# Small products in row and column groups, and the gate/up low-rank product added to the weights

## The chip, the cores and the metric

The kernel runs on one core of one Trainium2 chip. The metric is the device time of one execution in microseconds, of which the median of several runs is taken. One profiled execution gives the rows that are read here; its time is told beside its span.

## What is computed

The reference is two decoder layers on 8 x 128 = 1024 tokens of width 512, each step followed by a residual sum and a layer norm. Cut to what the change touches:

```python
# layer 1, "attention" (quantised weights with low-rank additions)
def _lin_lora(x, W, A, B):                 # A: (16, in), B: (out, 16)
    base = jnp.einsum('bsh,oh->bso', x, W)
    lora = jnp.einsum('bsr,or->bso', jnp.einsum('bsh,rh->bsr', x, A), B)
    return base + lora
q, k, v = (_lin_lora(x, _dequant(codes[n], scales[n]), A[n], B[n]) for n in range(3))
o  = _lin_lora((q + k + v) / 3.0, _dequant(codes[3], scales[3]), A[3], B[3])
x1 = x + o
g  = _lin_lora(x1, _dequant(codes_gu[0], scales_gu[0]), A[4], Bgu[0])   # 512 -> 1792
u  = _lin_lora(x1, _dequant(codes_gu[1], scales_gu[1]), A[5], Bgu[1])   # 512 -> 1792
h  = jax.nn.silu(g) * u
return x1 + _lin_lora(h, _dequant(codes_down, scales_down), A_down, B_down)
# layer 1, cross attention: scores = (x Wq^T + bq)(ctx Wk^T + bk)^T / sqrt(512), softmax, times ctx
```

Before it come layer 0 (an attention of eight heads of width 8, a softmax over the channels of the context, a linear layer with one of four low ranks chosen per token), and behind it the cross attention and a feed-forward layer with ternary weights.

## The kernel before

The 1024 tokens are eight tiles of 128 (NT = 8). Each engine has its own program, written out by hand in one order, and waits for counters (semaphores) that the others raise; what stands behind a waiting instruction in its engine's program waits as well. In the line numbers below L502 is the helper that transposes a token tile, L1023 ScalarE's copy of a transposed tile, L1430 VectorE's low half of it.

**Early parts.** The keys of the cross attention are prepared while the eight heads are worked on: `key_step` (L590 to L608) makes Wk^T Wq in four groups of four products and then two rows, bk Wq and bq Wk, each as four products with one output row, accumulated. In the next loop `key_bias` (L655) makes the bias row of the keys for half of the tokens, again four accumulated products of one output row and 512 columns; ScalarE copies it (L1141), and one DMA writes it out. In the third loop `attention_lora` (L732) makes the low-rank part of the four attention weights, two products a step (48 rows of contraction for q, k, v together, 16 for o), and VectorE adds each (`add_lora`, L1570). Products of float32 operands are two instructions each in the trace.

**The token loop (L817).** Step t holds: `attention_out(t)` (L763, four products of 512 columns), the transposes of tile t - 1 from `rbuf` (L502), and two `down_lora` products (L804, contraction 16, 512 columns) that VectorE adds to the down weights in `fold` (L1672). VectorE's loop (L1639) adds x1 (L1646), takes the low half of the transposed tile (L1430), at step 0, 1, 2 and 5 joins and scales weights (L1359, L1365, L1377, L1600), at step 4 makes the first tile's low half (L1605), sums x1 (L1668) and makes its folds. From the second step on TensorE's `attention_out(t)` waits for the x1 sum two steps back, the transposes for the one before.

**The gate/up stage (L847 to L851).** It has 14 tiles (j) of 128 gate and 128 up columns, two buffers (s = j mod 2). ScalarE bends codes into values (L973 to L989), VectorE joins and scales them; ScalarE rounds the weights to float32r (`gu_hi`, L1166) and VectorE takes what is left (`gu_low`, L1605). TensorE then runs, for each half of the tokens (tg, 512 columns) and for gate and up, twelve products high x high, high x low, low x high, and one for the low rank:

```python
pe.matmul(dst, b_st[:, s, g * P:(g + 1) * P], th[:, cols], start=False, stop=True).then_inc(done, 1)
```

Its operand `th` is x1 A^T, made between the token loop and the first tile by `gu_lora` (L807, 24 products for both halves), rounded by ScalarE (L1186) and completed by VectorE (L1637). `b_st` is B, rounded tile by tile (L1170, L1610) from `b_gu`, which SyncE loads. ScalarE applies silu to the gate's bank (L1198), VectorE multiplies by the up bank (`hidden`, L1595). TensorE may overwrite a pair of banks (gate and up of one half) when the hidden product of four pairs before is done:

```python
pe.wait_ge(h_ready, 2 * j + tg + 1)     # four pairs of banks in turn, the count starts at 4
```

VectorE's order in a tile is `gu_rest` (join_below, scale), `hidden` of the tile two back, `gu_join_above` of the next tile, the low half of B, `gu_low`. The down product follows (L859), which uses banks 0 to 7 for the eight token tiles.

## Time and profile before

| what | us |
|---|---|
| median of 3 runs (739.55 to 745.03) | 739.68 |
| profiled execution, its own time | 739.51 |
| its span, first to last instruction | 737.7 |
| busy: TensorE, VectorE, ScalarE | 691.8, 398.7, 384.4 |

The busy shares tell which engine is short; the chain tells which work ended last, step by step backward. The duration of one product in the trace holds its way through the array, which overlaps with the next product, so the distance between starts is its price, not its duration. The granted clock is given as a share of full speed: 1.00 is 2.4 GHz and 0.50 is 1.2 GHz.

### The profile page before, as it was taken

The numbers are of one execution on the slowest core, as the hardware profiler recorded it, in microseconds if no ns is written. First come the engines' busy times: TensorE is split into PE (matmuls) and PEld (weight loads), VectorE is DVE, ScalarE is ACT, GpSimd is POOL, SyncE is SP. The second block draws the span as 40 slices with busy tenths as digits, with TensorE's granted clock in tenths as the row PEclk, the third lists the DMA queues.
The fourth block names the chain that finished last, engine by engine and source line by source line (L and its number), as shares of the span: only waits on it lengthen the run. The fifth ranks groups of instructions, "written<-read, shape, count | busy, mean of one in ns | idle before, by whom it ended". The sixth has DMA issues, their size and how long they took to land.

```text
span 737.7 us, 8504 instructions
## 1 busy us (share of the span) xinstructions
PE 691.8 (94%) x3196; PEld 480.7 (65%) x3196; DVE 398.7 (54%) x691; ACT 384.4 (52%) x553; POOL 66.9 (9%) x126
## 2 busy tenths in 40 slices
PE   5879999999999998999999999999997999999993
PEld 3545454544554446888888887888764888887872
DVE  3367776657556773665555623456677222223386
ACT  4456677945557506757575713444434333334653
POOL 1022213201112000000000000002122000000022
PEclk9889999999999799999999999999999999999997
DMA  5582095421123320332423000003450122210002
GB/s 154 200 295 80 3 283 168 135 71 58 61 60 112 92 63 18 107 104 85 122 77 115 5 1 0 1 1 114 157 230 28 58 58 85 66 50 0 0 29 85
DMA packets 24905, 63.32 MB, mean 86 GB/s; under 512 B 5471, under 2 KB 10143, under 8 KB 23970
## 3 DMA queue, kind: packets, MB, share of 16 engines
q1 hardware_dynamic: 24866, 62.79, 26.7%
q8 instruction: 25, 0.41, 0.2%
q14 instruction: 14, 0.11, 0.0%
HBM read 58.06 MB, written 4.72 MB: 85 GB/s over the span
## 4 chain that ended last, share of the span: by engine, by line
PE 84%; DVE 7%; ACT 4%; issue 2%; DMA 2%; POOL 1%; SPq 1%; POOLq 0%; DVEq 0%; ACTq 0%
PE bank L859 16%; PE bank L842 7%; PE bank L843 7%; PE bank L844 7%; PE bank L928 7%; PE bank L929 7%; PE bank L722 4%; PE bank L763 4%; PE bank L652 3%; PE bank L502 2%; PE bank L750 2%; PE bank L845 2%; PE bank L804 2%; PE bank L602 1%; PE bank L578 1%
## 5 line engine op out<-in xcount | busy, mean ns | idle before, releaser
L981 ACT ACTIVATE line<-line 128x1024 f32<-128x1024 f32 x87 | 91.1, 1048 | 0.1
L928 PE MATMUL bank<-xh,wh 128*128 128x512 f32 x224 | 88.4, 395 | 1.5 <-issue 1.5
L859 PE MATMUL bank<-wh,xh 128*128 128x512 f32 x224 | 87.8, 392 | 2.0 <-DVE xl L1689 1.8
L842 PE MATMUL bank<-xh,wh 128*128 128x512 f32 x224 | 87.8, 392 | 1.4 <-DVE th L1637 1.4
L929 PE MATMUL bank<-xl,wh 128*128 128x512 f32 x224 | 88.1, 393 | 0.0
L843 PE MATMUL bank<-xl,wh 128*128 128x512 f32 x224 | 87.5, 391 | 0.0
L859 PE MATMUL bank<-wh,xl 128*128 128x512 f32 x224 | 87.4, 390 | 0.0
L844 PE MATMUL bank<-xh,wl 128*128 128x512 f32 x224 | 87.4, 390 | 0.0
L1332 POOL TENSOR_SCALAR rstd<-mv 128x1 f32<-128x1 f32 x45 | 20.0, 445 | 650.7 <-DVE mv L1703 474.9
L1222 ACT ACTIVATE xh<-arena 128x512 fp32r<-128x512 f32 x56 | 35.4, 632 | 68.5 <-PE bank L859 59.8
L1689 DVE TENSOR_TENSOR xl<-arena,xh 128x512 fp32r<-128x512 f32 x56 | 38.5, 688 | 52.5 <-ACT xh L1222 52.3
L1789 DVE SCALAR_TENSOR_TENSOR arena<-bank,ff_s,arena 128x512 f32<-128x512 f32 x28 | 21.0, 751 | 79.1 <-PE bank L929 77.7
L1595 DVE TENSOR_TENSOR arena<-arena,bank 128x512 f32<-128x512 f32 x28 | 19.2, 685 | 60.3 <-PE bank L845 60.3
L859 PEld LDWEIGHTS bank<-wh,xh 128*128 128x128 f32 x224 | 42.0, 188 | 13.0 <-DVE xl L1689 3.3
L928 PEld LDWEIGHTS bank<-xh,wh 128*128 128x128 f32 x224 | 42.6, 190 | 10.5 <-issue 1.7
L842 PEld LDWEIGHTS bank<-xh,wh 128*128 128x128 f32 x224 | 42.2, 188 | 10.9 <-DVE th L1637 1.9
L929 PEld LDWEIGHTS bank<-xl,wh 128*128 128x128 f32 x224 | 42.6, 190 | 8.9
L843 PEld LDWEIGHTS bank<-xl,wh 128*128 128x128 f32 x224 | 42.2, 189 | 9.1
L844 PEld LDWEIGHTS bank<-xh,wl 128*128 128x128 f32 x224 | 42.0, 188 | 9.2
L859 PEld LDWEIGHTS bank<-wh,xl 128*128 128x128 f32 x224 | 42.1, 188 | 8.6
L1198 ACT ACTIVATE arena<-bank 128x512 f32<-128x512 f32 x28 | 16.6, 591 | 57.8 <-PE bank L845 57.8
L1359 DVE SCALAR_TENSOR_TENSOR line<-line 128x1024 f32<-128x1024 f32 x29 | 35.3, 1216 | 18.5 <-ACT line L989 18.4
(183 smaller groups left out, 1202.6 us busy)
## 6 DMA issues: line engine op xcount, KB each, us to landing
codes<-in_c_gu SPq DMA_DIRECT2D x14, 512.0 KB, 3.9
scales<-in_s_gu SPq DMA_DIRECT2D x28, 256.0 KB, 3.8
codes<-in_t_gu SPq DMA_DIRECT2D x14, 512.0 KB, 3.6
codes<-in_c_dn SPq DMA_DIRECT2D x7, 512.0 KB, 4.8
scales<-in_s_dn SPq DMA_DIRECT2D x14, 256.0 KB, 3.9
fold<-in_t_dn SPq DMA_DIRECT2D x1, 3584.0 KB, 13.3
codes<-in_c_qkv SPq DMA_DIRECT2D x6, 512.0 KB, 4.9
arena<-in_xT SPq DMA_DIRECT2D x4, 512.0 KB, 4.9
```

The costliest lines, as they stand in the source:

```text
L722: pe.matmul(bank[FF_BANK[b % 3]][:, :], xT[:, k, b * P:(b + 1) * P], w0T[:, k, :], start=(k == 0), stop=False)
L763: last = pe.matmul(turn_bank(t)[:, :], xT[:, k, t * P:(t + 1) * P], mT[k], start=(k == 0), stop=(k == KD - 1))
L842: pe.matmul(dst, wh[:, s, c:c + P], xh[:, k, cols], start=(k == 0), stop=False)
L843: pe.matmul(dst, wh[:, s, c:c + P], xl[:, k, cols], start=False, stop=False)
L844: pe.matmul(dst, wl[:, s, c:c + P], xh[:, k, cols], start=False, stop=False)
L859: last = pe.matmul(bank[b][:, :], h[:, s, b * P:(b + 1) * P], wp[:, s, 0:D], start=first and p == 0, stop=last_one and p == len(parts) - 1)
L928: pe.matmul(dst, wh[:, s, c:c + P], xh[:, k, cols], start=(k == 0), stop=False)
L929: last = pe.matmul(dst, wh[:, s, c:c + P], xl[:, k, cols], start=False, stop=(k == KD - 1))
L981: nc.scalar.activation(below(slot), below(slot), ACT.Prelu, bias=bias, scale=scale, alpha=alpha).then_inc(bent, 1)
L1222: nc.scalar.activation(xh[:, s, cols], hT[:, slice(j, j + 1), cols].rearrange("p o t -> p (o t)"), ACT.Copy).then_inc(done, 1)
L1359: nc.vector.scalar_tensor_tensor(weight(slot), weight(slot), FAR_NEAR, near(slot), ALU.add, ALU.max).then_inc(joined, 1)
L1689: return nc.vector.tensor_tensor(xl[:, s, cols], hT[:, slice(j, j + 1), cols].rearrange("p o t -> p (o t)"), f32(xh[:, s, cols]), ALU.subt ...
```

## The change

**Gate and up.** `th`, `b_st`, `ah`, `al` and all their steps are gone. In their place TensorE makes the low-rank weights themselves, A^T B of a tile (`gu_lora(j)`): four float32 products with 32 rows of contraction and 256 columns, in row groups 0 and 1, into banks 2 and 3. VectorE adds both banks to the scaled weights in one step (`gu_lora_add`, in `gu_rest`) before they are rounded, and ScalarE's rounding waits for the addition. Tiles 0 and 1 have theirs in steps 1 and 4 of the token loop, the others at the head of the tile before. Since banks 2 and 3 are taken, three pairs of banks go in turn (`pair_bank`), and a pair waits for the hidden product of three pairs before. `late_bank` turns the bank numbers of all that follows by two.

**Down fold.** Three `down_lora` products a step lie in three row groups (steps 0 to 4; before, two a step in steps 0 to 6) and wait together for all folds of the step before. **Attention.** The two `attention_lora` products of a step are one for q, k, v in rows 0 to 63 and one for o in rows 64 to 127. **Key rows.** The products of one output row in `key_step` and `key_bias` go to four column groups and are no longer accumulated; the copy takes 128 rows, and the four parts are summed later by a product with `picked` or with `ones` of four rows. The bias row is written by four DMAs in place of one.

```diff
+GU_LORA = (1, GU1_STEP - 1)
-X3_BANK = (7, 4)
+X3_BANK = (1, 6)
+PAIR_BANK = (0, 4, 6)
...
+        lora_ps = heads_ps[:, 0:2, :]
+        def pair_bank(p, g):
+            return bank[PAIR_BANK[p % len(PAIR_BANK)] + g][:, :]
+        def late_bank(n):
+            return bank[(n + 2) % len(bank)]
...
@@ SyncE
+            for c in range(KD):
+                sp.dma_start(beta_dram[c:c + 1, :], beta_s[c * ROWG:c * ROWG + 1, :]).then_inc(kb_out, 16)
...
                     sp.dma_start(codes[:, slot, :],
                                  i["c_gu"][slice(j, j + 1), :, :].rearrange("o p c -> (o p) c")).then_inc(in_gu[s], 16)
+                    if j >= 2:
+                        sp.wait_ge(lora_made, j - 1)
+                    sp.dma_start(b_gu[:, s, :], i["b_gu"][j]).then_inc(in_bgu[s], 16)
                     sp.wait_ge(scaled, C_GU + j - RING + 1)
...
-                    sp.wait_ge(b_ready, j + 1)
-                    sp.dma_start(b_gu[:, s, :], i["b_gu"][slice(j, j + 1), :, :].rearrange("o r c -> (o r) c")).then_inc(in_gus[s], 16)
@@ TensorE: key_step, key_bias
-                    last = pe.matmul(bank[0][0:1, :], k_b[:, d:d + 1], wq1[:, d, :], start=(d == 0), stop=(d == KD - 1))
+                    last = pe.matmul(bank[0][d * ROWG:d * ROWG + 1, :], k_b[:, d:d + 1], wq1[:, d, :], start=True, stop=True)
...
-                    last = pe.matmul(bank[7][0:1, :], wb[:, KD + c:KD + c + 1], ctxT[:, g, c, :], start=(c == 0), stop=(c == KD - 1))
+                    last = pe.matmul(bank[7][c * ROWG:c * ROWG + 1, :], wb[:, KD + c:KD + c + 1], ctxT[:, g, c, :], start=True, stop=True)
@@ attention_lora
-                if n >= 2:
-                    pe.wait_ge(af_added, n - 1)
-                j = n % KD
-                rows = slice(0, 3 * R1) if n < KD else slice(O_ROW, O_ROW + R1)
+                j, o = divmod(n, 2)
+                if n >= 2 and not o:
+                    pe.wait_ge(af_added, n)
+                rows = slice(o * O_ROW, (o + 1) * O_ROW)
@@ down_lora, gu_lora, token loop
-                if j >= 3:
-                    pe.wait_ge(fold_kept, j - 2)
-                rows = slice(QR * (j // DT), QR * (j // DT) + R1)
+                if j >= 3 and j % 3 == 0:
+                    pe.wait_ge(fold_kept, j)
+                rows = slice(QR * (j % 3), QR * (j % 3) + R1)
...
-            def gu_lora(tg):
-                pe.wait_ge(a_ready, 1)
-                pe.wait_ge(xl_ready, NT // 2 * (tg + 1))
-                for k in range(KD):
-                    for a, xs in ((ah, xh), (ah, xl), (al, xh)):
-                        last = pe.matmul(bank[2 + tg][0:3 * RG, :], a[:, k, :], xs[:, k, tg * 512:(tg + 1) * 512],
-                                         start=(k == 0 and a is ah and xs is xh), stop=(k == KD - 1 and a is al))
-                last.then_inc(t_ps, 1)
+            def gu_lora(j):
+                pe.wait_ge(in_bgu[j % 2], 16 * (j // 2 + 1))
+                if j == 0:
+                    pe.wait_ge(in_agu, 16)
+                    pe.wait_ge(ln_sum, 3 * NT)
+                else:
+                    pe.wait_ge(lora_added, j)
+                for h in range(2):
+                    for n in range(2):
+                        rows = slice(n * RG, (n + 1) * RG)
+                        last = pe.matmul(lora_ps[:, n, h * 2 * P:(h + 1) * 2 * P], a_gu[rows, h, :], b_gu[rows, j % 2, :], start=True, stop=True)
+                last.then_inc(lora_made, 1)
...
-                for j in range(2 * t, min(2 * t + 2, NF)):
+                for j in range(3 * t, min(3 * t + 3, NF)):
                     down_lora(j)
-                if t == NT - 1:
-                    gu_lora(0)
-            gu_lora(1)
+                if t in GU_LORA:
+                    gu_lora(GU_LORA.index(t))
@@ gu_tile
                 pe.wait_ge(w_ready, j + 1)
-                pe.wait_ge(b_ready, j + 3)
+                if 1 <= j < NF - 1:
+                    gu_lora(j + 1)
...
-                    pe.wait_ge(h_ready, 2 * j + tg + 1)
+                    p = TG * j + tg
+                    if p == 0:
+                        pe.wait_ge(xl_ready, NT // 2)
+                    elif p == 1:
+                        pe.wait_ge(xl_ready, NT)
+                        pe.wait_ge(fold_kept, NF)
+                    else:
+                        pe.wait_ge(h_ready, p + 2)
...
-                        pe.matmul(dst, b_st[:, s, g * P:(g + 1) * P], th[:, cols], start=False, stop=True).then_inc(done, 1)
@@ ScalarE
-                if t == 2:
-                    act.wait_ge(in_agu, 16)
-                    nc.scalar.activation(ah[:, :, :], aT_gu, ACT.Copy).then_inc(a_hi, 1)
...
-                act.wait_ge(scaled, C_GU + j + 1)
+                act.wait_ge(lora_added, j + 1)
                 nc.scalar.activation(wh[:, s, :], weight(gu_slot(s)), ACT.Copy).then_inc(hi_ready, 1)
@@ VectorE
+            def gu_lora_add(s, j):
+                dve.wait_ge(lora_made, j + 1)
+                dve.wait_ge(scaled, C_GU + j + 1)
+                w = weight(gu_slot(s)).rearrange("p (h i c) -> p i h c", h=2, i=2)
+                nc.vector.tensor_tensor(w, w, lora_ps.rearrange("p i (h c) -> p i h c", h=2), ALU.add).then_inc(lora_added, 1)
...
                 gu_scale(s, n)
+                gu_lora_add(s, j)
...
-                gu_lora_low(s, j)
...
-                for j in range(2 * b, min(2 * b + 2, NF)):
+                for j in range(3 * b, min(3 * b + 3, NF)):
                     dve.wait_ge(fold_ready, j + 1)
```

## Rows read from the trace of the kernel before

**Rows 1.** The page: busy time, share and instructions; the chain by engine.

```profile
PE 691.8 (94%) x3196; PEld 480.7 (65%) x3196; DVE 398.7 (54%) x691; ACT 384.4 (52%) x553; POOL 66.9 (9%) x126
...
PE 84%; DVE 7%; ACT 4%; issue 2%; DMA 2%; POOL 1%; SPq 1%; POOLq 0%; DVEq 0%; ACTq 0%
```

**Rows 2.** Windows view, gate/up stage: busy us of each engine and count, clock, DMA.

```profile
286.00:453.00 167.00, 166.36 (x727) 136.89 (x728) 84.75 (x92) 102.47 (x130) 0.00 (x0) 1.00 0.24 70
```

**Rows 3.** Timeline, TensorE in the first tile: start us, us, engine, line, operands.

```profile
289.27 0.39 PE L844 MATMUL bank<-xh,wl 128*128 128x512 f32 x1
...
289.50 0.40 PE L845 MATMUL bank<-th,b_st 96*128 96x512 f32 x1
...
289.73 0.40 PE L842 MATMUL bank<-xh,wh 128*128 128x512 f32 x1
```

**Rows 4.** Timeline, TensorE between the token loop and the first tile.

```profile
276.93 0.60 PE L502 MATMUL bank<-ident,rbuf 128*128 128x128 f32 x4
...
277.29 0.48 PE L813 MATMUL bank<-xh,ah 128*96 128x512 f32 x1
...
286.64 0.50 PE L842 MATMUL bank<-xh,wh 128*128 128x512 f32 x1 [1.40 <-DVE th L1637]
```

**Rows 5.** Timeline around the first key_bias: TensorE, then ScalarE's idle time behind it.

```profile
116.90 3.59 PE L660 MATMUL bank<-project,wb 128*1 128x512 f32 x8
...
120.43 1.12 PE L637 MATMUL bank<-heads,prob 128*128 128x512 f32 x2
...
125.02 0.69 ACT L1113 ACTIVATE heads<-bank,wb 128x512 f32<-128x512 f32 x1 [3.19 <-PE bank L652]
```

**Rows 6.** Timeline, small float32 products in column groups (L567), then row groups (L539).

```profile
58.31 0.62 PE L567 MATMUL bank<-fold 128*32 128x128 f32 x16
58.87 0.73 PE L539 MATMUL bank<-heads 9*128 9x128 f32 x16
59.52 1.98 PE L602 MATMUL bank<-arena 128*128 128x512 f32 x4
```

**Rows 7.** Timeline, one step of the token loop: transposes, down products, attention_out.

```profile
264.98 0.60 PE L502 MATMUL bank<-ident,rbuf 128*128 128x128 f32 x4
...
265.51 1.98 PE L804 MATMUL bank<-arena 16*128 16x512 f32 x4
...
267.42 3.70 PE L763 MATMUL bank<-arena 128*128 128x512 f32 x8
```

**Rows 8.** Timeline, VectorE in the token loop: two folds, scale, addition.

```profile
236.17 1.27 DVE L1672 TENSOR_TENSOR fold<-fold,bank 128x512 f32<-128x512 f32 x2
...
250.24 1.22 DVE L1600 SCALAR_TENSOR_TENSOR line<-line,scales 128x1024 f32<-128x1024 f32 x1
...
251.38 0.68 DVE L1668 TENSOR_TENSOR x<-x,rbuf 128x512 f32<-128x512 f32 x1
```

**Rows 9.** Timeline, VectorE in a gate/up tile: hidden product and low half.

```profile
310.81 0.69 DVE L1595 TENSOR_TENSOR arena<-arena,bank 128x512 f32<-128x512 f32 x1 [3.80 <-PE bank L845]
...
313.89 1.23 DVE L1605 TENSOR_TENSOR wl<-line,wh 128x1024 fp32r<-128x1024 f32 x1
```

**Rows 10.** The page: granted clock in 40 slices; windows view of one stretch.

```profile
PEclk9889999999999799999999999999999999999997
...
240.00:244.00 4.00, 4.00 (x6) 1.71 (x6) 3.12 (x5) 1.47 (x2) 0.00 (x0) 0.50 0.32 94
```

**Rows 11.** Timeline, one attention_lora step (two products, four instructions).

```profile
161.38 1.98 PE L741 MATMUL bank<-heads,arena 48*128 48x512 f32 x4
```

**Rows 12.** Timeline, the rounding of A for gate and up, TensorE behind.

```profile
51.71 0.56 DVE L1517 TENSOR_TENSOR al<-fold,ah 128x384 fp32r<-128x384 f32 x1 [0.55 <-ACT ah L1097]
...
53.46 0.44 PE L546 MATMUL bank<-ident,fold 128*128 128x128 f32 x2 [1.08 <-DVE fold L1465]
```

**Rows 13.** Timeline, key_step with the seventh token tile, and VectorE's maximum.

```profile
85.29 1.88 PE L604 MATMUL bank<-arena,k_b 128*1 128x512 f32 x4
...
86.04 1.21 DVE L1465 TENSOR_REDUCE fold<-bank 128x8 f32<-128x1024 f32 x1
```

More of the change, by code:

```diff
@@ L139, in decoder_kernel @@
         wl = sb("wl", [P, 2, CH], F32R)
[L140 to L146 removed]
+        b_gu = sb("b_gu", [2 * RG, 2, 2 * P])
+        a_gu = sb("a_gu", [2 * RG, 2, P])
+        folded_m = sb("folded", [P, T])
         ff_s = sb("ff_s", [P, 2, 2])
@@ L286, in decoder_kernel @@
         in_gus = [sem(f"in_gu_scales{n}") for n in range(2)]
+        in_bgu = [sem(f"in_b_gu{n}") for n in range(2)]
         in_ctx1, in_kq, in_wk, in_wq, in_ds = sem("in_context1"), sem("in_kq"), sem("in_wk"), sem("in_wq"), sem("in_ds")
@@ L1437, in _ @@
             nc.vector.memset(lmT[RMAX:RMAX + 1, :, :], 1.0)
-            link(nc.vector.memset(ones[:, :], 1.0))
+            nc.vector.memset(wb[:, 2 * KD:2 * KD + 1], 0.0)
+            nc.vector.memset(ones[:, :], 1.0)
+            link(nc.vector.memset(picked[:, :], 0.0))
+            for c in range(KD):
+                nc.vector.memset(picked[c * ROWG:c * ROWG + 1, :], 1.0)
             for g in range(HG):
@@ L1871, in layout @@
         "s_o": pairs(sa[3].T.reshape(KD, 2, D)), "lora_l": lora_l, "lora_r": lora_r,
-        "aT_gu": rows(np.tile(A[4:6].reshape(RG, D).T, 3)), "b_gu": b_gu, "a_d": a_d, "bT_d": bT_d,
+        "a_gu": c(A[4:6].reshape(RG, 2, 2, P).transpose(2, 0, 1, 3).reshape(2 * RG, 2, P)), "b_gu": b_gu, "a_d": a_d, "bT_d": bT_d,
         "c_gu": wide(f["L1_attn_codes_gu"][0], f["L1_attn_codes_gu"][1]),
```

135 lines of the change are left out of this document (49 added, 86 removed).

## The prediction

> **What bounds the kernel now.** I read the page's busy shares first, then its chain: TensorE is busy 94% of the span and holds 84% of the chain that ended last, the other engines about half busy [rows 1]. So a step is worth what it takes off TensorE's queue, or off a wait in which TensorE stands. Then I read the stages. In the gate/up stage 727 products are recorded in 167.0 us with 166.36 busy [rows 2]: nothing but TensorE limits it. The duration printed for one product (0.39 to 0.40 us) is no price, since products overlap: starts lie 0.23 apart [rows 3]. 166.36 / 727 = 0.2288 us each is the price I use; with 0.395 the removed product would look worth 22.1 us in place of 12.8.
>
> **Prices of small float32 products.** A float32 product is two instructions. Eight of them, 512 columns each, take 116.90 to 120.43 [rows 5], so 0.44 apiece, and so 0.22 for 256 columns (half the columns). Where small products already lie in groups, sixteen instructions of 128 columns in four row groups go from 58.87 to the next product at 59.52, 0.65 us, and sixteen in column groups from 58.31 to 58.87, 0.56 us [rows 6]; one behind the other they would take 16 x 0.11 = 1.76. So groups do run beside each other here. The change uses two, three or four groups, and 256 or 512 columns, which no row shows; between full overlap (the longest one counts) and none (they add up) I take full overlap, as rows 6 are nearest.
>
> A switch between whole-array and grouped products costs something. Four transposes before a whole-array product start 0.36 ahead of it [rows 4]; before the 16-row products of the down fold they start 0.53 ahead, so 0.17 goes into the switch; behind it four instructions take 265.51 to 267.42, 1.91 for 4 x 0.44 = 1.76, so 0.15 comes out [rows 7]. A visit to grouped mode costs 0.32. The Trainium skill, page "TensorEngine Tiling (Array Packing)", section Key Properties, says that changing the tiling mode drains TensorE, without a figure, which speaks against visits in the middle of a dense stream; the rows agree with 0.32 a visit, and a sum with no drain would come out 12 x 0.32 = 3.8 us lower.
>
> **Gate/up stage.** Removed: L845, 56 products x 0.2288 = 12.8 us. Added at the head of tiles 1 to 12: one visit with two halves of two row groups, 4 x 0.22 + 0.32 = 1.20 us, x 12 = 14.4 us (no overlap at all: 8 x 0.22 + 0.32 = 2.08, 25.0 us; no drain and full overlap: 0.88, 10.6 us). The stage becomes 1.6 us longer, between 2.2 shorter and 12.2 longer. It gains nothing by itself.
>
> A tile is then 48 x 0.2288 + 1.20 = 12.2 us. New waits: VectorE adds the low-rank tile from PSUM (1024 columns; 512 cost about 0.64 in a pair [rows 8], so 1.25) only after the visit for it, at the start of the tile before; behind that wait on VectorE's queue lie the two hidden products of the tile two back, join_above and gu_low; on ScalarE gu_hi waits for the addition. From the start of a tile: visit done 1.3, addition 2.6, hidden products 3.3 and 4.0, ScalarE's rounding 3.7, join_above 5.2, gu_low (1.23 [rows 9]) 6.5. Who waits: TensorE's second pair, which with three pairs of banks in turn needs the hidden product of three pairs before, at 1.2 + 5.5 = 6.7 (there at 3.3), and the next tile at 12.2 (there at 6.5). Slack 3.4 and 5.7 us, and VectorE idles 3.8 before a hidden product today [rows 9]; ScalarE loses 0.4 a tile with b_st. I cost these waits at nothing. SyncE's b_gu load now waits for the visit two tiles back, a tile ahead of its use; nothing.
>
> **Between the token loop and the first tile.** Now the last transposes are at 276.93, half of the x-by-A products from 277.29, and the tile stream starts at 286.64, behind the second half and the rounding of it on ScalarE and VectorE [rows 4]. All of that goes. But the token loop before is rearranged too, so I laid it out again, in the clock of this trace, with attention_out 8 x 0.44 = 3.5, transposes 0.4, VectorE's additions 0.64 to 0.69 and its 1024-wide steps 1.22 [rows 7, 8]. Down products now come in threes (0.88 + 0.32 a step in place of 1.91 + 0.17), and a step's three wait for all folds of the step before. Step 0 runs three from 234.5; VectorE's folds of step 0 end 238.1 (three, from 236.17 [rows 8]), and TensorE waits 1.9 us for them; then three products and gu_lora(0), attention_out(2) at 240.2 as today. VectorE's step 1 (three additions, one scale, three folds) ends 244.0; its step 2 holds both joins, the scale, the new addition and three folds, and ends 253.0. TensorE's fourth group waits for that from 249.3: 3.7 us idle. Then attention_out(4) to 257.5, two products and gu_lora(1), attention_out(5) to 263.5. VectorE's step 5 with the second tile's weights ends 271.0, steps 6 and 7 carry two additions and x_low each, the last transposes are at 274.4, and the stream starts at 274.9. It needs only half of xl there; the other half is wanted 5.5 us later and is there in 1.5. Tile 1's weights: ScalarE's four bends and rounding end 280.7, VectorE 282.2, wanted 285.9; covered.
>
> So 286.64 - 274.9 = 11.7 us, if the clock stays at 2.4 GHz. Today it is at 1.2 GHz (0.50) for all of 240 to 244 and falls twice in 237 to 258 by the page's digits [rows 10]; the first fall follows 16-row products and small waits. With idle stretches of 1.9 and 3.7 us I keep one fall of 3.4 us, which costs 1.7: 10.0 us gained. Bounds 6 (waits as laid out, two long falls) and 12.
>
> **Earlier parts.** key_bias, twice: eight instructions in 3.53 [rows 5] become four column groups in 2 x 0.44 + 0.32 = 1.20, 2.33 saved each. TensorE goes straight on into context and keys; ScalarE, next latest, idles 3.19 behind it today [rows 5]: 4.7 us, bounds 2.3 and 5.3. attention_lora, four times: four instructions in 1.9 [rows 11] become two in time, 0.88 saved each, switches unchanged: 3.5 us, bounds 0 and 3.5; VectorE's work in a step (about 7.1) is near TensorE's new period but not above it. The rounding of A at 51: VectorE's part, waiting for ScalarE's, ends at 52.2 and TensorE idles 1.08 for the row maximum behind it [rows 12]: 1.0 saved, bounds 0 and 1.1. key_step's last two groups: four instructions take 1.88 [rows 13], but behind them TensorE waits for VectorE's maximum, done 87.25, so the first pair saves nothing; the second saves some 0.6, and the single ones pay about as much for switches: 0, bounds -1 and +1. The copies of 128 rows in place of 1 have the same columns; three more SyncE issues for beta, the memsets and the turned bank numbers have slack: nothing.
>
> **Sum.** -1.0 - 4.7 - 3.5 - 10.0 + 1.6 = -17.6 us. The profiled execution took 739.51 (span 737.7 and 1.8 around it), the median of the runs shown is 739.68: 739.5 - 17.6 = 721.9 us.
>
> **Rivals.** (a) The visits in the tile stream overlap badly (256 columns with a weight load in the same row group each time), the rest as forecast: +10.6, 732.5. For it: no row shows it with two groups; against it: rows 6. (b) Slower: groups do not overlap at these column counts anywhere. Then gate/up is 12.2 longer, key_bias is longer by a switch (0.6 in all), attention_lora saves nothing, and the token loop loses four of its ten: -1.0 + 0.6 - 6.0 + 12.2 = +5.8, 745.3. It decides from the point where less than about a quarter of the overlap is there (the overlap is worth 23.4 us in all, and 5.8 of that is missing for a draw). Against it stand both rows of grouped products [rows 6]. (c) VectorE's blocked queue: if the hidden product behind the addition came 3.4 us later than laid out, the second pair would wait; each further microsecond costs 12. At 1 us over: 734. (d) The token loop gives less: VectorE and TensorE in lockstep with two clock falls, 726. (e) More: fewer falls also around 155 and 180 and no drain in the stream, 714.
>
> **Chances.** Forecast 0.58, (a) 0.12, (b) 0.03, (c) 0.04, (d) 0.15, (e) 0.08. The range takes in forecast, (d) and (e) with their bounds and leaves out (b), (c) and the end of (a): 713 to 731. A change within 1% (732.1 to 747.1) is about what a measurement of this kernel cannot tell from none. Faster by over 1%: forecast, (d), (e) and half of (a) and more, 0.90; within 1%: 0.08; slower: 0.02.
>
> **What would show it.** Groups of the visit: four pairs of starts some 0.22 apart, and 1.2 between the products around them, else (a). Starts of tiles 12.2 apart, with no wait for a hidden product (else c). The tile stream starting 11.7 or 10 us earlier against attention_out(0), with TensorE waits for the folds near its second and fourth group. L660's successor about 1.2 behind it. The prediction is wrong if the gate/up stage is not within 164 to 179 us, or if VectorE makes the token loop longer than laid out.

## The result, and the profile after

The median after the change is 721.09 us (720.24 to 722.53, four runs), before it 740.06 on the same chip; the ratio is 0.9735, with a 95% interval of 0.9696 to 0.9774. Faster by 2.65%, 0.8 us from the forecast of 721.9 and inside the range. The profiled execution took 721.29 (span 719.5); before it was 739.51 (737.7), so 18.2 us are to be found. Of all executions reported in this document one stood far from the others of its kernel (key_bias_row, 1723.13 us), and no ratio counts it.

The page first. TensorE still holds 81% of the chain [rows 1 had 84%], so marks on its queue split the difference. The clock row ends in a 7 in both kernels: in the last 8.6 us (before) and 9.3 us (after) of the span TensorE has no product left and its granted clock is 1.2 GHz.

```profile
PE 668.8 (93%) x3228; PEld 468.4 (65%) x3228; DVE 404.9 (56%) x694; ACT 379.6 (53%) x536; POOL 66.9 (9%) x126
PEclk9979999999999899999999999999999999999997
PE 81%; DVE 8%; ACT 4%; issue 2%; DMA 2%; POOL 1%; SPq 1%; POOLq 0%; DVEq 0%; ACTq 0%
```

Then the stretches between the marks, kernel after. A row gives the stretch and its length, then the busy time of TensorE, of its weight loads, of VectorE, ScalarE and GpSimd, then the granted clock and the DMA traffic. The marks are the first of the single-row key products (L612), the two key_bias, attention_lora, attention_out(0), the first product of the gate/up stream and the first down product:

```profile
79.40:117.40 38.00, 35.16 (x240) 18.93 (x240) 28.89 (x50) 28.92 (x42) 8.78 (x12) 0.96 0.65 194
117.40:141.10 23.70, 23.70 (x99) 13.05 (x97) 16.39 (x36) 21.44 (x35) 7.62 (x14) 1.00 0.44 145
141.10:155.20 14.10, 12.47 (x49) 5.86 (x48) 8.68 (x26) 8.48 (x13) 1.61 (x4) 1.00 0.36 113
155.20:215.20 60.00, 59.27 (x210) 30.17 (x209) 38.32 (x125) 36.89 (x51) 7.14 (x19) 1.00 0.24 72
215.20:268.40 53.20, 45.05 (x150) 20.65 (x148) 42.25 (x57) 23.36 (x28) 3.95 (x4) 0.90 0.25 73
268.40:436.30 167.90, 167.90 (x770) 133.44 (x769) 90.95 (x92) 100.20 (x118) 0.00 (x0) 1.00 0.23 67
```

The stretch from attention_out(0) to the stream, which this text calls the loop, was this in the kernel before:

```profile
226.50:286.60 60.10, 57.08 (x157) 25.74 (x155) 42.38 (x59) 25.93 (x33) 3.93 (x4) 0.91 0.24 66
```

The clock column has to be read before the lengths. Up to that last idle end, TensorE's granted clock is 1.2 GHz in both kernels for stretches of 3.4, 6.8 or 10.2 us and 2.4 GHz otherwise; a product takes twice as long there (starts of the down products of down_one_group lie 0.85 apart at 1.2 GHz and 0.43 at 2.4), so 3.4 us at the lower level cost about 1.7. Kernel before, then kernel after, for their low stretches behind 79 us (before had 20.4 us there, after 13.6; ahead of 79 us both have 13.6):

```profile
155.60:159.00 3.40, 3.40 (x7) 1.58 (x6) 2.89 (x14) 0.00 (x0) 0.00 (x0) 0.50 0.53 158
179.50:182.90 3.40, 3.40 (x7) 1.33 (x6) 3.19 (x16) 1.93 (x3) 1.11 (x3) 0.50 0.00 0
237.50:244.30 6.80, 6.80 (x9) 2.50 (x8) 4.16 (x6) 3.97 (x5) 0.00 (x0) 0.50 0.24 66
254.60:258.00 3.40, 3.40 (x5) 1.35 (x4) 1.65 (x3) 0.83 (x1) 0.00 (x0) 0.50 0.09 19
572.00:575.40 3.40, 3.40 (x10) 2.62 (x9) 0.75 (x1) 1.15 (x4) 0.00 (x0) 0.50 0.00 0
```

```profile
99.20:102.60 3.40, 3.40 (x5) 1.35 (x4) 3.29 (x6) 1.95 (x4) 0.00 (x0) 0.50 0.90 318
228.90:232.30 3.40, 3.40 (x5) 1.34 (x6) 3.40 (x6) 1.30 (x2) 0.00 (x0) 0.50 0.28 77
242.50:249.30 6.80, 5.86 (x11) 2.29 (x12) 4.56 (x8) 1.58 (x2) 0.00 (x0) 0.50 0.30 93
```

"At equal clock" below is a length less half of its low-clock time (the idle end is left as it is). That is exact where TensorE is busy throughout, and somewhat too much where it is not.

| stretch, from mark to mark | before | after | at equal clock | term forecast |
|---|---|---|---|---|
| start to first key product | 79.3 | 79.4 | 72.5 to 72.6 | -1.0 |
| to first key_bias | 37.6 | 38.0 | 37.6 to 36.3 | 0 |
| to second key_bias | 26.2 | 23.7 | 26.2 to 23.7 | -2.35 |
| to attention_lora | 18.3 | 14.1 | 16.6 to 14.1 | -2.35 |
| to attention_out(0) | 65.1 | 60.0 | 63.4 to 60.0 | -3.5 |
| to the stream | 60.1 | 53.2 | 55.0 to 48.1 | -10.0 |
| gate/up stream | 166.7 | 167.9 | 166.7 to 167.9 | +1.6 |
| rest | 284.4 | 283.2 | 282.7 to 283.2 | 0 |

Lengths are good to 0.1, as the marks are rounded. The stretches sum to -18.2, the terms to -17.6. Of these 3.4 us are falls of the clock, three gone (at 155.6, 179.5 and 572) and one new (at 99.2), so at equal clock the change is worth 14.8 in this pair of executions; over all executions it is 16.2 (the table at the end of the experiments).

A visit (the four grouped products of `gu_lora` between whole-array products), timeline of TensorE, kernel after (start, duration):

```profile
291.30 0.39 PE L864 MATMUL bank<-xh,wl 128*128 128x512 f32 x1
291.62 1.13 PE L826 MATMUL bank<-b_gu,a_gu 32*128 32x256 f32 x8
292.68 0.50 PE L862 MATMUL bank<-xh,wh 128*128 128x512 f32 x1
293.02 0.39 PE L863 MATMUL bank<-xl,wh 128*128 128x512 f32 x1
```

From 291.30 to 292.68 are 1.38 us, and the next product comes 0.34 behind in place of 0.23: the visit is worth 1.38 + 0.34 - 2 x 0.23 = 1.26, against 1.20 forecast. Its eight instructions start in four pairs, at 291.62, 291.94, 292.16 and 292.37, and tiles start 12.17 apart (280.51, 292.68), both about as laid out. Twelve visits would add 15.1 us, and the stream grew by 1.2, so the 56 removed products were worth 13.9, or 0.25 each in place of 0.2288: the starts next to them lay 0.23 to 0.24 apart, where the rest of the stream runs at 0.227.

The token loop, kernel after, same view:

```profile
223.22 1.13 PE L812 MATMUL bank<-arena 16*128 16x512 f32 x6
224.29 0.66 PE L510 MATMUL bank<-ident,rbuf 128*128 128x128 f32 x4
226.84 1.13 PE L812 MATMUL bank<-arena 16*128 16x512 f32 x6 [1.89 <-DVE fold L1668]
227.80 1.03 PE L826 MATMUL bank<-b_gu,a_gu 32*128 32x256 f32 x8
228.76 5.40 PE L771 MATMUL bank<-arena 128*128 128x512 f32 x8
...
243.44 2.08 PE L812 MATMUL bank<-arena 16*128 16x512 f32 x6 [3.72 <-DVE fold L1668]
245.45 5.62 PE L771 MATMUL bank<-arena 128*128 128x512 f32 x8
...
265.85 0.63 PE L510 MATMUL bank<-ident,rbuf 128*128 128x128 f32 x4 [1.04 <-DVE xl L1435]
267.98 0.63 PE L510 MATMUL bank<-ident,rbuf 128*128 128x128 f32 x4 [1.51 <-DVE xl L1435]
268.36 0.48 PE L862 MATMUL bank<-xh,wh 128*128 128x512 f32 x1
```

The 24 products by A and the wait behind them are gone, where the kernel before had them from 277.29 to 286.64 [rows 4]; this end of the loop is called the exit below. In their place the step groups wait for VectorE's folds: 1.89 and 3.72 us. The attention_out behind the first wait takes 5.40, behind the second 5.62, where the same eight instructions elsewhere take 3.6: those are the two stretches at 1.2 GHz.

### The profile page after: what moved, and what is told of

It is laid out like the page before. It is cut to its first block, busy times and chain, and to the rows that moved or that the text cites. A ratio compares the mean times of both kernels' runs of the same rounds, so it can differ in the third digit from the quotient of the medians.

```text
span 719.5 us, 8570 instructions
## 1 busy us (share of the span) xinstructions
PE 668.8 (93%) x3228; PEld 468.4 (65%) x3228; DVE 404.9 (56%) x694; ACT 379.6 (53%) x536; POOL 66.9 (9%) x126
## 4 chain that ended last, share of the span: by engine, by line
PE 81%; DVE 8%; ACT 4%; issue 2%; DMA 2%; POOL 1%; SPq 1%; POOLq 0%; DVEq 0%; ACTq 0%
PE bank L877 16%; PE bank L862 7%; PE bank L864 7%; PE bank L863 7%; PE bank L946 7%; PE bank L947 7%; PE bank L730 4%; PE bank L660 4%; PE bank L510 2%; PE bank L771 2%; PE bank L826 2%; PE bank L758 2%; PE bank L610 2%; PE bank L575 1%; PE bank L586 1%
## 5 line engine op out<-in xcount | busy, mean ns | idle before, releaser
L946 PEld LDWEIGHTS bank<-xh,wh 128*128 128x128 f32 x224 | 42.0, 188 | 10.3 <-issue 1.7
L1617 DVE TENSOR_TENSOR line<-line,bank 128x1024 f32<-128x1024 f32 x14 | 17.1, 1221 | 54.3 <-PE bank L826 54.1
L1292 ACT ACTIVATE arena<-bank,ff_s 128x512 f32<-128x512 f32 x28 | 19.3, 690 | 47.8 <-PE bank L947 47.8
```

Source lines behind the costliest of these rows:

```text
L946: pe.matmul(dst, wh[:, s, c:c + P], xh[:, k, cols], start=(k == 0), stop=False)
```

## The experiments

Theory of the gain: grouped products run fully beside each other, a visit costs 0.32 beside the products, and what the loop gains is the exit, less the waits that the order of VectorE's work brings. Rivals: the gain came from the clock; or the gate/up rewrite carries the whole of it; or the small groups do (key rows, key_bias, attention_lora and down fold). Twelve kernels were run in three jobs, each beside the kernel before (medians 739.26, 739.82 and 739.75).

**1. gu_one_group.** All four products of a visit in one row group.

```diff
-                        rows = slice(n * RG, (n + 1) * RG)
+                        rows = slice(0, RG)
...
-                        last = pe.matmul(lora_ps[:, n, h * 2 * P:(h + 1) * 2 * P], a_gu[rows, h, :], b_gu[rows, j % 2, :], start=True, stop=True)
+                        last = pe.matmul(lora_ps[:, n, h * 2 * P:(h + 1) * 2 * P], a_gu[rows, 2 * h + n, :], b_gu[rows, j % 2, :], start=True, stop=True)
```

> All four products of gu_lora(j) read rows 0 to 31, so they lie in one row group; nothing else changes. Theory (products in two row groups run beside each other at 256 columns, and a visit is 4 x 0.22 + 0.32 = 1.2 us): a visit becomes 8 x 0.22 + 0.32 = 2.1 us, the twelve tiles 0.86 to 0.9 longer each, 10.4 us in all, so 731 to 732. The visit takes 2.1 us between the products around it and eight starts lie 0.215 apart. Rival (the visit is bound by something else, its weight loads or the switch): within 2 us of the changed kernel, 721 to 723.

Measured 736.35 us, ratio 0.9961 (0.9943 to 0.9978). The visit and the stream in its trace, TensorE's timeline and the window:

```profile
295.17 0.39 PE L864 MATMUL bank<-xh,wl 128*128 128x512 f32 x1
295.49 1.99 PE L826 MATMUL bank<-b_gu,a_gu 32*128 32x256 f32 x8
297.41 0.50 PE L862 MATMUL bank<-xh,wh 128*128 128x512 f32 x1
```

```profile
269.70:449.70 180.00, 180.00 (x771) 143.27 (x770) 91.03 (x92) 100.39 (x118) 0.00 (x0) 0.99 0.21 63
```

A visit takes 2.24 from start to start, 0.86 more than the 1.38 of the kernel after: exactly the four slots of 0.215 that no longer lie beside others. 12 x 0.86 = 10.3, and one fall of the clock in the stream (0.99) is the rest of its 12.1 us. Overlap of two row groups is full, and it decides here: without it 721 becomes 736. The total missed its expectation by 4 to 5 us: the two visits in the loop are 1.7, the fall in the stream 1.7, and the loop has 13.6 us of low clock in place of 10.2, another 1.7. Against them stand 3.4 us less of it ahead of 79 us; the profiled execution (734.71) was the fastest of ten, so these lengths explain its 13.4 above the kernel after, and the median's 15.3 but for 1.9. The rival, within 2 us of the kernel after, is out.

**2. gu_order.** The row group in the outer loop, the halves in the inner one: 0, 0, 1, 1 in place of 0, 1, 0, 1.

```diff
-                for h in range(2):
-                    for n in range(2):
+                for n in range(2):
+                    for h in range(2):
```

> The same four products in the same two row groups, issued group 0, group 0, group 1, group 1 in place of 0, 1, 0, 1. Theory A (TensorE starts instructions in program order, and one that must wait for its row group holds back those behind it): only the change of group overlaps, seven slots of 0.215 in place of four, 0.65 us more a visit, 7.7 us in all, 729. Theory B (instructions of the free group are taken ahead from the queue): four slots as now, 721.

Measured 723.87 us, 0.9781 (0.9748 to 0.9814). Timeline of a visit in this kernel:

```profile
293.91 0.39 PE L864 MATMUL bank<-xh,wl 128*128 128x512 f32 x1
294.23 1.14 PE L826 MATMUL bank<-b_gu,a_gu 32*128 32x256 f32 x8
295.30 0.50 PE L862 MATMUL bank<-xh,wh 128*128 128x512 f32 x1
```

It is 1.39 from start to start, as with alternating groups, and the stream takes 168.0. The first two instructions start at 294.23 and 294.24, where two of one group lie at least 0.215 apart; so the first of the second group, the fifth to be issued, starts with the very first, and theory B holds in the trace. Overlap does not need neighbours from different groups: the products of the free group start ahead. The total is 2.8 above the kernel after with the same lengths in the stream; its loop spent 13.6 us at 1.2 GHz, 1.7 us dearer, and about 1 us is open.

**3. only_gu.** The kernel after, with key rows, key_bias, attention_lora and the down fold as before: the gate/up part alone.

```diff
-                for j in range(3 * t, min(3 * t + 3, NF)):
+                for j in range(2 * t, min(2 * t + 2, NF)):
                     down_lora(j)
                 if t in GU_LORA:
                     gu_lora(GU_LORA.index(t))
```

> The changed kernel with key_step, key_bias, attention_lora and the down fold as before (two down products a step, one row group, steps 0 to 6). Theory (the gate/up part gains by what stood between the token loop and the stream, not in the stream): the 8.9 us between the last transposes and the stream go, the rounding of A goes (up to 1.0), the stream is 1.3 longer, the two visits and two additions in the token loop cost 1 to 3: 732 to 736. Rival (the 56 removed products carry the gain): the stream itself shorter by some 10 us and the total below 729.

Measured 739.41 us, 1.0002 (0.9979 to 1.0025): nothing in the total, and a miss of the expectation. The window of the loop and part of TensorE's timeline in it:

```profile
226.40:286.60 60.20, 56.59 (x149) 25.03 (x148) 42.18 (x57) 23.34 (x28) 3.92 (x4) 0.86 0.22 65
```

```profile
236.89 1.57 PE L811 MATMUL bank<-arena 16*128 16x512 f32 x3
237.85 0.83 PE L825 MATMUL bank<-b_gu,a_gu 32*128 32x256 f32 x2
238.28 1.03 PE L811 MATMUL bank<-arena 16*128 16x512 f32 x1
239.11 1.91 PE L825 MATMUL bank<-b_gu,a_gu 32*128 32x256 f32 x6
240.95 5.75 PE L770 MATMUL bank<-arena 128*128 128x512 f32 x8
...
254.80 1.56 PE L811 MATMUL bank<-arena 16*128 16x512 f32 x2 [1.48 <-DVE fold L1667]
256.28 6.62 PE L770 MATMUL bank<-arena 128*128 128x512 f32 x8
```

Its loop is as long as before, though the 24 products by A and the exit's wait are gone. The clock is 0.86, with 17.0 us at the lower level: at equal clock the stretch is 51.7, 3.3 less than before, and the stream is 1.2 longer. So the part does gain some 2 to 3 us and loses them to the clock; the table below shows the same over ten executions. TensorE waits 1.48 and 0.63 for folds. VectorE's additions of the low-rank tile (1.22 each) stand in that queue ahead of the folds.

**4. only_small.** The opposite: the kernel before, with the groups of the small products.

```diff
-                for j in range(2 * t, min(2 * t + 2, NF)):
+                for j in range(3 * t, min(3 * t + 3, NF)):
                     down_lora(j)
                 if t == NT - 1:
                     gu_lora(0)
```

> The kernel before with the groups of key_step, key_bias, attention_lora and the down fold of the change, and gate/up as before (th, b_st, L845). Theory: key_bias 4.7, attention_lora 3.5, and in the token loop 3 to 5 of the 8 us that TensorE saves, since it then waits for VectorE's folds: 727 to 731. Rival (TensorE's savings are swallowed by waits behind them): 735 to 740. If the parts add up, the gains of this one and of the gate/up part alone make 19 us within 3.

Measured 722.49 us, 0.9771 (0.9725 to 0.9816), better than expected (727 to 731) and 1.4 above the whole change, which lies inside the spread of both (720.1 to 724.2 and 720.2 to 722.5). Its loop:

```profile
213.30:268.20 54.90, 47.71 (x158) 22.49 (x156) 42.23 (x59) 26.01 (x33) 3.94 (x4) 0.94 0.25 73
```

At equal clock 51.5, against 55.0 before and 48.1 after. So at equal clock the down groups are worth 3.5 and the gate/up part another 3.4 in the loop, of which the stream takes back 1.2. The expectation left out the 1.3 us of the key rows, and clock: the loop has 6.8 us at the lower level in place of 10.2, and the falls around 155 and 180 are absent.

**5. down_one_group.** The three down products of a step in one row group.

```diff
-                rows = slice(QR * (j % 3), QR * (j % 3) + R1)
+                rows = slice(QR * (j // 3 % 4), QR * (j // 3 % 4) + R1)
```

> The changed kernel with the three down products of a step in one row group, so one behind the other. By the sum: 0.88 x 2 more in steps 0 to 3 and 0.88 in step 4 on TensorE, 7.9 us, of which the waits for VectorE's folds cover some 3.5: 4.4 us more, 725 to 726. Rival (VectorE sets the loop, the groups save nothing there): 721.

Measured 728.61 us, 0.9862 (0.9817 to 0.9906), against 721.1 for the change. The first three products, TensorE's timeline of this kernel:

```profile
223.70 2.84 PE L813 MATMUL bank<-arena 16*128 16x512 f32 x6
226.47 0.66 PE L510 MATMUL bank<-ident,rbuf 128*128 128x128 f32 x4
```

They take 2.77 from start to start where the kernel after has 1.07 (223.22 to 224.29): 1.70 are four slots of 0.43, so three groups overlap fully. The loop at equal clock is 52.8 against 48.1, +4.7 where +4.4 was expected. Of the other 2.8 us of the median, 1.7 are low clock in its loop (13.6 us in place of 10.2).

**6. key_bias_row.** key_bias as before, accumulated in one output row.

```diff
-                    last = pe.matmul(bank[7][c * ROWG:c * ROWG + 1, :], wb[:, KD + c:KD + c + 1], ctxT[:, g, c, :], start=True, stop=True)
+                    last = pe.matmul(bank[7][0:1, :], wb[:, KD + c:KD + c + 1], ctxT[:, g, c, :], start=(c == 0), stop=(c == KD - 1))
```

> The changed kernel with key_bias accumulated in one output row as before (four products behind each other, one row copied, one DMA, the scores' bias from one row). By the sum 2.33 us twice: 4.7 more, 725.8. Rival (ScalarE takes over as the next wait and covers half): 723 to 724.

Measured 725.35 us, 0.9797 (0.9768 to 0.9826). Timeline of the instructions in question, in this kernel and then in the kernel after:

```profile
114.37 3.59 PE L667 MATMUL bank<-project,wb 128*1 128x512 f32 x8
117.90 1.12 PE L644 MATMUL bank<-heads,prob 128*128 128x512 f32 x2
```

```profile
117.45 1.04 PE L668 MATMUL bank<-project,wb 128*1 128x512 f32 x8
118.42 1.13 PE L645 MATMUL bank<-heads,prob 128*128 128x512 f32 x2
```

3.53 became 0.97 from start to start; the stretches of this kernel are 26.2 and 16.6 where the kernel after has 23.7 and 14.1: 5.0 for the pair, 4.7 forecast. Six slots of 0.43 are 2.6, so the four column groups overlap fully at 512 columns.

**7. att_rows.** attention_lora as before, every product in its own time.

```diff
-                j, o = divmod(n, 2)
-                if n >= 2 and not o:
-                    pe.wait_ge(af_added, n)
-                rows = slice(o * O_ROW, (o + 1) * O_ROW)
+                if n >= 2:
+                    pe.wait_ge(af_added, n - 1)
+                j = n % KD
+                rows = slice(0, 3 * R1) if n < KD else slice(O_ROW, O_ROW + R1)
```

> The changed kernel with attention_lora as before: the two products of a step in one row group (48 rows for q, k, v in steps 0 and 1, 16 rows for o in steps 2 and 3), each waiting for its own addition. By the sum 0.88 x 4 = 3.5 more, 724.6, all of it between the first attention_lora and the first attention_out (63.5 us in place of 60.0 at full clock). Rival (VectorE's step of 7.1 us was the next bound and half of it had stayed covered): 723 or less.

Measured 727.70 us, 0.9848 (0.9805 to 0.989). Its window, with a fall of the clock in it (0.97):

```profile
154.30:219.40 65.10, 64.37 (x210) 32.23 (x209) 38.23 (x124) 36.96 (x51) 7.09 (x19) 0.97 0.22 66
```

63.4 at equal clock against 60.0 in the kernel after: 3.4, as forecast (3.5). The total is 3.2 us worse than that. Its loop, whose code is that of the kernel after, has 13.6 us of low clock in place of 10.2, and over the four executions the low-clock time is 43.6 against 36.3, which is 3.6 us of time.

**8 to 12: the order in the token loop.** If TensorE's waits for folds give back what the exit saves, an earlier fold must bring it. *folds_first* lets VectorE do x1's sum and the folds ahead of a step's weight work (`tile_weights`, from step 1 on). *folds_first_late* also moves the second tile's weights from step 5 to step 8. *visits_first* puts gu_lora ahead of the down products in the steps that have both. *last_bank* gives the last tile's transposes a bank of their own, so that they don't wait for xl (ScalarE's copy and VectorE's low half read that bank too). Each is built on the one before; the four edits, in that order:

```diff
-                u = PLAN_END[3] + b
...
-                    gu_rest(1, 1, 0)
+                def tile_weights():
+                    u = PLAN_END[3] + b
...
+                        gu_rest(1, 1, 0)
+
+                if b == 0:
+                    tile_weights()
                 if b < NT:
                     dve.wait_ge(x1_ready, b + 1)
                     nc.vector.tensor_tensor(x[:, b, :], x[:, b, :], rbuf[:, s, :], ALU.add).then_inc(x1_sum, 1)
...
+                if b > 0:
+                    tile_weights()
```

```diff
-                    elif b == GU1_STEP:
+                    elif b == NT:
```

```diff
+                if t in GU_LORA:
+                    gu_lora(GU_LORA.index(t))
                 for j in range(3 * t, min(3 * t + 3, NF)):
                     down_lora(j)
-                if t in GU_LORA:
-                    gu_lora(GU_LORA.index(t))
```

```diff
+                    if t == NT:
+                        pe.wait_ge(fold_kept, NF)
-                    if t >= 2:
+                    elif t >= 2:
                         pe.wait_ge(xl_ready, t - 1)
-                    transpose_tile(t - 1, rbuf[:, (t - 1) % 2, :], bank[6])
+                    transpose_tile(t - 1, rbuf[:, (t - 1) % 2, :], bank[7 if t == NT else 6])
```

> The changed kernel, but in steps 1 to 8 of VectorE's token loop the x1 sum and the folds come ahead of the weights' joins, scale and addition. Theory (TensorE's 3.7 us wait for the folds of step 2 is a matter of order on VectorE, and long waits bring clock falls behind them): that wait goes, from attention_out(0) to the stream 48 to 50 us in place of 53.2, total 716 to 718. Rival 1 (the clock falls anyway, for the small products themselves): 719 to 720. Rival 2 (VectorE's work is the bound, the wait moves to the x1 sum): no gain, 721.

> As folds_first, and the second tile's weights (join, join, scale, addition) go from step 5 of VectorE's token loop to step 8, behind the last transposes; they are wanted 11 us later. Theory (in the last steps TensorE waits for VectorE's x1 sum and x_low, 1.0 and 1.5 us in the changed kernel): 2 us less than folds_first, 714 to 716. Rival (the second tile's weights are then late): the stream waits ahead of tile 1, 718 or more.

> folds_first_late with gu_lora ahead of the three down products in steps 1 and 4 of TensorE's token loop, so that it runs while the folds are waited for (1.89 and 1.67 us there). Theory: 0.96 each is covered, 1.9 us less than folds_first_late's 717.0: 715. Rival (gu_lora(1) then waits for the addition of tile 0's, which VectorE now does late): 717 or more.

> visits_first with the last tile's transposes in bank 7, free since the last fold, so that they need not wait for x_low of the tile before. Theory: the last wait, 1.50 us, shrinks to that for the x1 sum: 0.7 to 1.5 us less than visits_first, 714. Rival (the x1 sum comes as late, since VectorE sets the end): no difference.

| kernel | median | ratio (95%) | loop | at equal clock |
|---|---|---|---|---|
| folds_first | 719.54 | 0.9731 (0.970 to 0.9763) | 50.4 | 47.0 |
| folds_first_late | 717.02 | 0.9688 (0.9662 to 0.9714) | 49.1 | 45.7 |
| visits_first | 713.61 | 0.9652 (0.9619 to 0.9686) | 45.8 | 44.1 |
| last_bank | 712.94 | 0.9644 (0.9613 to 0.9676) | 44.7 | 43.0 |

Each step shortens the loop. folds_first missed its expectation (716 to 718) by 1.5 us: a fall of the clock at 265.1 lengthened its stream to 169.6. Its total is what its rival 1 gave (719 to 720, the clock falls all the same), and its loop of 50.4, with 6.8 us of low clock, just misses the 48 to 50 of the theory. folds_first_late is 2.5 below it (2 expected), visits_first 3.4 below that (1.9 expected). last_bank differs from visits_first in its median by less than the spread of either, though its loop is 1.1 shorter at equal clock. TensorE's timeline of last_bank:

```profile
225.49 1.13 PE L826 MATMUL bank<-b_gu,a_gu 32*128 32x256 f32 x8
227.44 1.13 PE L812 MATMUL bank<-arena 16*128 16x512 f32 x6 [0.83 <-DVE fold L1674]
228.51 5.40 PE L771 MATMUL bank<-arena 128*128 128x512 f32 x8
...
240.47 3.70 PE L771 MATMUL bank<-arena 128*128 128x512 f32 x8
...
246.78 1.13 PE L812 MATMUL bank<-arena 16*128 16x512 f32 x4 [0.61 <-DVE fold L1674]
```

The wait of 1.89 is 0.83, that of 3.72 is gone, a new one of 0.61 stands at the fifth group, and of the second low-clock stretch nothing is left. The first is: the attention_out from 228.51 takes 5.40 behind a wait of 0.83 as it did behind 1.89. The total is 8 us less than the change, 27 less than before. It is the best version found.

The last kernel, *small_folds_first*, is only_small with the folds first.

> only_small (gate/up as before) with the x1 sum and folds ahead of the weights in VectorE's token loop. Theory A (the gate/up part is worth its 3.4 us at equal clock also here): its 4.3 us of waits for folds go and 2 to 3 us are gained, 719 to 721, still 2 to 4 above folds_first_late with both parts. Theory B (the gate/up part is worth nothing once the loop is in order): 717 or less, as low as folds_first_late.

Measured 719.88 us (717.29 to 723.43), 0.9741 (0.9694 to 0.9789), as theory A has it; loop 51.7, at equal clock 50.0. With folds first on both sides the gate/up part is 50.0 to 47.0 in the loop, less the stream's 1.2: about 2 us, as in the order of the change. The medians (719.88 and 719.54, from different jobs) do not show it, for the falls lie unevenly.

**All executions at equal clock.** Every execution has its span and its mean granted clock. The span times the clock is the span less half of its low-clock time (the idle end counts here), so falls can be taken out of each execution and not only of the profiled one. The clock is given to 0.001, which is 0.4 us either way. The executions of the kernel after are those of the first section, the others those of the three jobs. Means, with the lowest and highest execution:

| kernel | executions | low-clock time, us | span x clock, us |
|---|---|---|---|
| before, all three jobs | 32 | 40.4 (29.3 to 46.0) | 717.5 (716.1 to 719.0) |
| after | 4 | 36.3 (36.0 to 37.4) | 701.3 (699.7 to 702.7) |
| gu_one_group | 10 | 41.1 (39.6 to 42.7) | 713.7 (713.0 to 714.7) |
| gu_order | 4 | 39.0 (36.0 to 40.4) | 702.1 (701.8 to 702.8) |
| only_gu | 10 | 46.0 (42.7 to 50.3) | 714.6 (713.9 to 715.7) |
| only_small | 4 | 33.9 (28.8 to 40.5) | 703.6 (702.2 to 705.2) |
| down_one_group | 4 | 41.5 (39.2 to 46.8) | 706.5 (706.2 to 707.1) |
| key_bias_row | 3 | 32.8 (31.9 to 33.3) | 707.0 (706.5 to 708.0) |
| att_rows | 4 | 43.6 (40.6 to 46.6) | 704.1 (703.0 to 704.7) |
| folds_first | 4 | 35.2 (31.6 to 43.3) | 700.7 (699.3 to 701.5) |
| folds_first_late | 4 | 32.5 (30.0 to 34.3) | 698.8 (697.8 to 699.3) |
| visits_first | 4 | 28.5 (27.0 to 29.9) | 697.5 (696.9 to 697.9) |
| last_bank | 4 | 28.8 (28.4 to 29.8) | 696.7 (695.8 to 698.0) |
| small_folds_first | 4 | 30.2 (25.8 to 36.1) | 703.2 (702.6 to 703.9) |

One and the same kernel before has 29.3 to 46.0 us of low clock, so where and how often the clock falls is not fixed by the program alone, and the falls of one profiled execution are not those of the kernel. Without them the executions of a kernel lie within 3 us, and the columns settle three questions. The change is worth 16.2 us at equal clock and 2.0 by fewer falls, so the gain did not come from the clock. The gate/up part alone gains 2.9 (only_gu), its ranges apart from those of before; beside the small groups it is worth 2.3, and with folds first 2.5. The small groups alone gain 13.9, most of it, and the two parts (16.8) make the whole. Against the kernel after, gu_one_group is 12.4 longer, down_one_group 5.2, key_bias_row 5.7 and att_rows 2.8, where the stretches gave 12.0, 4.7, 5.0 and 3.4. The four reorderings take 4.6 off at equal clock, and 3.8 by low-clock time that falls from 36.3 to 28.8; last_bank and visits_first are not told apart.

## Why the prediction was right, and where it was not

**Prices of grouped products: right.** Full overlap with two row groups of 256 columns (experiment 1: 0.86 a visit), with three of 512 (experiment 5: 4.7 against 4.4), with four column groups (experiment 6) and with two groups in attention_lora (experiment 7: 3.4 against 3.5). Rivals (a) and (b) are out. The price of a visit, with 0.32 from the switches of the kernel before [rows 7], held in the middle of the stream: 1.26 against 1.20. As its four slots are 0.86, the switches are 0.40 there.

**Gate/up stage: right.** +1.6 forecast, +1.2 measured; both of its terms were a little small (a visit 1.26, not 1.20; a removed product 0.25, not 0.2288), and the errors cancel. No wait for a hidden product occurs in it (TensorE is busy for all of 167.90), so rival (c) is out.

**key_bias: right.** -4.7 forecast, -5.0 measured, -2.5 each.

**Token loop: the waits were right, the clock was not.** The layout at 2.4 GHz gave 48.4 from attention_out(0) to the stream; measured at equal clock are 48.1, and both waits for folds came where they were put (1.9 and 3.7 laid out, 1.89 and 3.72 measured). What failed is the step "I keep one fall of 3.4 us, which costs 1.7": 10.2 us at 1.2 GHz stayed, as many as before, and the stretch became 6.9 us shorter in place of 10.0. The term was oversized by 3.1, and the result lies nearer to rival (d), which gave the loop 5.9 with two falls. Experiments 8 to 12 show that the waits were the place to work on: with both nearly gone the low-clock time in the loop was 3.4, and over the whole span of last_bank it was 28.4 to 29.8 against 36.0 to 37.4 in the kernel after.

**Early parts: two small misses.** The rounding of A, -1.0 forecast, does not show at the next mark (79.3 and 79.4, with 13.6 us of low clock ahead of both). At its own place the wait of 1.08 for VectorE [rows 12] is gone, but TensorE then waits 0.28 for ScalarE: from the sixteen products of 128 columns ahead (48.73 before, 49.36 after) to the product behind (53.73 and 53.70) it is 5.00 before and 4.34 after, 0.66 less. The kernel after was 0.63 behind when it came there, and why is open; this first stretch varies between 72.4 and 74.0 at equal clock among the kernels run here. The key rows, forecast 0, saved 1.3 at equal clock: the last group takes 3.25 (92.97 to 96.22) where it took 4.2 before, since the two single rows no longer accumulate one behind the other.

**The sum was closer than its terms.** Against -17.6 stand -18.2. The loop gave 3.1 less than forecast, the first stretch 1.1, attention_lora and the end 0.6 (4.8 in all); the key rows, key_bias and the stream gave 2.0 more; and falls of the clock outside the loop gave 3.4 more (three gone, one new). Put otherwise, the forecast was 14.2 at equal clock and 3.4 by fewer falls in the loop; measured in this pair of executions are 14.8 and 3.4, but not one of these falls went in the loop. The argument had no way to place them, so that the total was hit within 1 us is partly luck: the low-clock time over all executions moved experiments 2, 5 and 7 by 1.4, 2.6 and 3.6 us against the kernel after. Rival (e) had named the falls around 155 and 180, and both are gone; it was right in that part, and wrong in the stream without a drain.

**What each part of the change is worth** (at equal clock, shown by experiments 3 to 7 and the table over all executions): the small groups in the early parts some 10, the down groups 3.5, the gate/up part 3.4 in the loop less 1.2 in the stream. Before the runs I had counted the exit's 11.7 us as the gate/up part's; alone it gave 2.9 at equal clock and nothing in the total (experiment 3), because visits, two additions and the waits behind them take most of it back, and the clock the rest.

## What to carry to other kernels

Price a product by the distance of starts in a dense stretch, and products in separate row or column groups by the longest of them, plus the switches of one visit (0.3 to 0.4 here); two rows of the kernel before were enough for that. When the array gets faster, ask which slower engine's queue now stands ahead of the results it needs: putting folds ahead of work wanted later, with a visit moved into a wait and a bank of its own for the last tile, was worth another 8 us (4.6 at equal clock), more than the gate/up rewrite itself (2.3). Read the clock row before comparing two lengths, and compare them at equal clock; a single total hides errors of a few microseconds that cancel. The span times the mean clock does it for executions that were not profiled.

## What the runs showed of the hardware

Products of a free row group start ahead of earlier ones that wait for theirs. In only_gu two gate/up instructions (L825, start 237.85) begin ahead of the last down instruction (L811, 238.28), which the program issues first; and the order 0, 0, 1, 1 costs the same 1.39 us from start to start as 0, 1, 0, 1. The Trainium skill, page "TensorE: Matmul & The Clock Gate", section Part 3 (The mechanism), says that products start and end strictly in program order. By that rule the visit of gu_order would take seven slots of 0.215 (four of the first group, then three more of the second behind the one that they share), 0.65 more than the four slots measured, and that of the kernel after five; the starts in this case's traces disagree with it. Ends are modelled in these records, but counters are not, and on ends the traces agree with it: the last product issued raises `lora_made`, and in only_gu it starts at 239.71, ahead of two earlier ones of the other group (239.97 and 240.39), yet the counter rises at 241.05, 0.03 behind the modelled end of the latter. down_one_group shows it again (start 259.66, others until 259.98, counter at 260.39). So one counter on the last product still stood for all of them in these runs.

A float32 product is two instructions (eight for four products), and with two groups all eight take the time of four: 1.06 us to the next product in the kernel after (291.62 to 292.68), 1.92 in gu_one_group (295.49 to 297.41).

TensorE fell to 1.2 GHz in the loop with no idle stretch longer than 3.72 us ahead of the fall, and once behind only 1.89 us of idleness among 16-row products (L771 from 228.76); the kernel before fell at 237.5, amid its 16-row products, with no idle stretch of TensorE listed between 226 and that time. In kernels with shorter waits the low-clock time in the loop was 3.4 us (visits_first, last_bank) against 10.2 (after), 13.6 (gu_one_group, gu_order, down_one_group) and 17.0 (only_gu); but key_bias_row and att_rows have the loop of the kernel after, the same waits in it, and 13.6 us, so a difference of 3.4 between two of these loops says nothing. In visits_first and last_bank the fall that is left comes behind a wait of 0.83.

What sets off a fall outside the loop stays open. Ahead of the one at 155.6 before, TensorE was idle for 1.61 us (at 154.10), ahead of the one at 572 for 1.46 (at 571.69); but the kernel after has the same wait of 1.61 at 149.54 and keeps 2.4 GHz, and within 5 us of the falls at 99.2 (after) and 179.5 (before) there is no wait at all.
